# A two-pass graph kernel: the second pass's steps for loading, comparing, expanding and adding a block are set one or two turns nearer to its gather

## What is computed

```python
h = jnp.maximum(_layernorm(x, axis=-1), 0.0)
agg = jax.ops.segment_sum(h[src], dst, num_segments=h.shape[0])   # edges sorted by dst
x = x + jax.nn.relu(agg @ W.T + b)
```

## Time and profile before

| | |
|---|---|
| median of 3 runs | 1252.31 us (1250.37 to 1253.11) |
| profiled execution | 1251.71 us, of which the span is 1249.8 us |
| PE busy | 968.8 us (78%) |
| DVE busy | 1024.1 us (82%) |
| POOL busy | 784.5 us (63%) |
| ACT busy | 280.4 us (22%) |

### The profile page before, as it was taken

One profiled execution on the slowest core, in us unless ns is written; L12 is line 12 of the kernel. 1 busy time (PEld: TensorE's weight loads), 2 busy tenths in 40 slices (PEclk: granted clock), 3 DMA queues, 4 the chain that ended last, 5 costly groups with the idle time before them and its releaser, 6 DMA issues.

```text
span 1249.8 us, 20773 instructions
## 1 busy us (share of the span) xinstructions
PE 968.8 (78%) x5818; PEld 765.5 (61%) x5818; DVE 1024.1 (82%) x2720; ACT 280.4 (22%) x681; POOL 784.5 (63%) x836
## 2 busy tenths in 40 slices
PE   0122017999999999999999814888988989788988
PEld 0011014777777777777777613776776777676777
DVE  8888896899999999999999635677767777777874
ACT  1451032222222222222222111111112112111210
POOL 3000047777777777777778367777777777777750
PEclk9996556899999999999999855889898888989889
DMA  1000012788999899898897544778787777787765
GB/s 65 0 0 0 0 41 69 176 223 221 241 239 236 223 244 234 233 232 218 234 238 204 161 145 105 181 200 224 187 233 201 206 198 208 206 211 220 201 172 164
DMA packets 317563, 218.51 MB, mean 175 GB/s; under 512 B 223428, under 2 KB 255140, under 8 KB 317444
## 3 DMA queue, kind: packets, MB, share of 16 engines
q1 hardware_dynamic: 182100, 135.41, 38.6%
q10 hardware_dynamic: 110256, 62.42, 19.0%
q0 software_dynamic: 25088, 19.32, 8.7%
HBM read 137.51 MB, written 79.45 MB: 174 GB/s over the span
## 4 chain that ended last, share of the span: by engine, by line
DVE 47%; PE 16%; DMA 12%; POOL 9%; issue 7%; ACTq 6%; ACT 3%; DVEq 0%; POOLq 0%; SPq 0%
POOL xa L555 9%; DMA xa<-node_table,gi 7%; DVE feats L1077 7%; DVE feats L1075 7%; DVE oneh L1098 5%; DMA win<-records 4%; DVE dout L1117 4%; ACTq L679 4%; PE p_m L1364 3%; DVE kb L923 2%; DVE rec L1125 2%; DVE ka L923 2%; DVE shared L1098 2%; PE p_u L1376 2%; PE p_t L1376 2%
## 5 line engine op out<-in xcount | busy, mean ns | idle before, releaser
L536 POOL DMA_INDIRECT xa<-in_edge_attr_dram,gi x392 | 373.0, 952 | 232.2 <-issue 115.6
L555 POOL DMA_INDIRECT xa<-node_table,gi x392 | 370.1, 944 | 142.3 <-issue 103.1
L689 ACT ACTIVATE hid<-p_z,bias_z 128x512 f32<-128x512 f32 x98 | 113.5, 1158 | 239.3 <-issue 226.5
L1077 DVE TENSOR_TENSOR_SCAN feats<-c_rows,feats,p_g 32x512 f32<-32x512 f32 x97 | 123.3, 1271 | 1.4
L1075 DVE TENSOR_TENSOR_SCAN feats<-c_rows,feats,p_g 64x512 f32<-64x512 f32 x97 | 122.5, 1263 | 0.0
L1405 PE MATMUL p_g<-ident,hn 128*128 128x128 f32 x196 | 46.6, 325 | 97.4 <-DVE hn L1179 97.2
L742 ACT ACTIVATE sd<-mv,eps_t 128x4 f32<-128x4 f32 x98 | 29.2, 298 | 407.0 <-DVE mv L1170 350.0
L1098 DVE SCALAR_TENSOR_TENSOR shared<-p_m,node_of 112x1024 f32<-112x1024 f32 x98 | 117.2, 1196 | 3.8 <-PE p_u L1376 1.4
L1364 PE MATMUL p_m<-w_s,hid 128*128 128x64 f32 x784 | 109.3, 283 | 14.0 <-ACT hid L689 13.4
L1098 DVE SCALAR_TENSOR_TENSOR oneh<-p_m,node_of 112x1024 f32<-112x1024 f32 x98 | 119.3, 1217 | 0.2
L1381 PE MATMUL p_u<-one 128*128 128x512 f32 x230 | 115.9, 590 | 0.1
(11 more groups left out here) (257 smaller groups left out, 1577.1 us busy)
## 6 DMA issues: line engine op xcount, KB each, us to landing
win<-records SPq DMA_DIRECT2D x980, 28.9 KB
records<-rec ACTq DMA_DIRECT2D x196, 132.0 KB
din<-in_x_dram SPq DMA_DIRECT2D x49, 512.0 KB
node_table<-dout SPq DMA_DIRECT2D x49, 512.0 KB, 4.3
din<-node_table SPq DMA_DIRECT2D x43, 512.0 KB, 4.8
out_dram<-dout SPq DMA_DIRECT2D x43, 512.0 KB
c_rows<-rows_src ACTq DMA_DIRECT2D x141, 128.0 KB
win<-records ACTq DMA_DIRECT2D x588, 28.9 KB
```

The costliest lines, as they stand in the source:

```text
L536: g.indirect_dma_start(out=xa[n % XRING][:, t, 0:FE], out_offset=None, in_=edge_attr, in_offset=bass.IndirectOffsetOnAxis(ap=gi[0][:, BT * ...
L555: g.indirect_dma_start(out=xa[k % XRING][:, t, :], out_offset=None, in_=T, in_offset=bass.IndirectOffsetOnAxis(ap=gi[1][:, BT * n + t:BT * ...
L689: s.activation(hid[n % 2][:, :].rearrange("p (t n) -> p n t", n=P), p_z[n % 2][:, :].rearrange("p (n t) -> p n t", t=BT), ACT.Relu, bias=b ...
L1077: v.tensor_tensor_scan(f[64:96, :], c[64:96, at:at + BLK], p_g[n % 2][0:32, :], first[64:96], ALU.min, ALU.max).then_inc(feats_ok, 1)
```

## The change

Six of the distances change, and PE's turn is put in another order.

```diff
-DST_TAKE, DST_CONV, DST_REC, DST_WIN, DST_HOT, DST_EXP, DST_ADD, DST_PUT = 1, 2, 3, 6, 8, 9, 10, 12
+DST_TAKE, DST_CONV, DST_REC, DST_WIN, DST_HOT, DST_EXP, DST_ADD, DST_PUT = 1, 2, 3, 5, 7, 7, 8, 10
+DST_DIN = DST_ADD - 2
...
-                    if (n - DST_HOT) % 2 == 0 and valid(n - DST_HOT) and (n - DST_HOT) // 2 < ringed[1]:
-                        load_dense(1, (n - DST_HOT) // 2, T)
+                    if (n - DST_DIN) % 2 == 0 and valid(n - DST_DIN) and (n - DST_DIN) // 2 < ringed[1]:
+                        load_dense(1, (n - DST_DIN) // 2, T)
...
                 for n in range(BLOCKS + DST_EXP):
+                    if valid(n - DST_CONV):
+                        conv(n - DST_CONV)
+                    if valid(n):
+                        turn_h(n)
                     if valid(n - DST_EXP):
                         expand(1, n - DST_EXP)
                     if valid(n - DST_EXP) and valid(n - DST_EXP + 1):
                         pe.wait_ge(added, max(BLOCKS + n - DST_EXP + 1 - len(p_e[1]) + 1, BLOCKS))
                         stream(p_e[1][(n - DST_EXP + 1) % len(p_e[1])], BLK // 2)
-                    if valid(n - DST_CONV):
-                        conv(n - DST_CONV)
-                    if valid(n):
-                        turn_h(n)
```

## The result

The change made the kernel slower: 1265.73 us (median of 4 runs, 1257.96 to 1270.54) against 1252.7 us for the kernel before (four runs, where the table above has three), a ratio of 1.0107 with a 95% interval of 1.0069 to 1.0144. 1249.4 us had been forecast, in a range of 1246 to 1252.8; a slower kernel had been given one chance in ten. The profiled execution took 1265.09 us, its span is 1263.3 us against 1249.8.

A forecast was written before the change was run, and what follows sets the result against it. POOL's gathers, 1.249 us apart, were taken to pace the head and PE the tail. One expansion turn saved (-3.1) plus a tail loss (+0.2) made -2.9 us: 1249.4 us, range 1246 to 1252.8.

The forecast's parts named there:

- The tail: After the last gather, paced by PE: eight expansions left behind the last transposition, not nine, saving 3.1 us; 0.2 us lost.
- the second turn: Turn between PE's last expansion and DVE's addition: costs nothing today, so saves nothing.
- no loss for the last windows: Last windows at the pass's end, possibly held back by their records: loss between 0 and 2.0 us, taken as 0.2.
- the 35.9 given as a sign of being right: Stretch behind POOL's last gather: was to take 35.9 us, not 38.8, if the forecast was right.
- PE's moved expansion: One expansion done before the tail, about 6 us moved into PE's 94 us free in the head: cost nothing.
- the addition two turns sooner: DVE's addition, distance 10 to 8, may wait for PE's expansion: cost nothing, up to 10 us of lateness.
- the 2 us at a time: DVE's addition waiting for PE's expansion when PE is at its low clock: about 2 us.
- Windows a turn sooner: Window loads, distance 6 to 5: SP's data between 1.6 us early and 1.3 us late for the keys; cost taken as nothing.
- Dense loads and stores: The pair's load keeps two turns before its addition, the store two turns behind it: cost nothing.
- Rival C: Slower: DVE paces the head through new waits, 1268 us with 0.7 us of them a turn; chance 0.12.
- POOL's lead of 10 us: POOL's last gather came 10.3 us after the addition it needs; lateness up to 10 us was to cost nothing.

The follow-up runs named there:

- both cures: The changed kernel with the dense pair ahead of SP's windows and the dense store in another turn than the load: 1244.21 us, ratio 0.9965.
- experiment 1: The changed kernel with windows and one-hots at their distances of before (6, 8), addition at 9 and store at 11: 1249.85 us, ratio 1.0007.

## Why the prediction was wrong

*The tail* was right to a tenth: one expansion turn less, 3.1 us, the second turn worth nothing, no loss for the last windows. (Behind the last gather the changed kernel has 41.3 us, and not the 35.9 given as a sign of being right, nearly all of it the 5.1 us of lateness that PE brings along from the head.) In the kernel with both cures (1244.21, ratio 0.9965) the forecast of -2.9 us, a ratio of 0.9977, lies within the interval.

*PE's moved expansion* and *the addition two turns sooner*: cost nothing, as predicted: in the kernel with both cures POOL's 391 steps take 488.3 us (716.4 to 1204.7). DVE did wait for PE, 16.2 us between 850 and 1190, within the 2 us at a time that were worked out; experiment 1 shows that it is free.

*Windows a turn sooner* is the step that failed, in the sentence "I take nothing", together with *Dense loads and stores: Nothing*. It was seen that SP would be released by the record and not by the expansion of m-4. Only SP's windows were then followed, to find that they would be in time, and they were. What stands behind them in SP's queue was not followed: the dense pair, whose own waits had not changed but whose queue had. It was shifted onto ACT's windows, in every second turn, where before it met them at varying distances. The prediction had put a cost of 0 there; the runs show about 22 us in the head (17.0 in POOL's row, 5.1 behind its last gather). The load of the pair is also the sixth of the "six distances" of the change, from turn 8 to turn 6; it and the store kept their places in SP's turn, and that was read as keeping their times.

*Rival C* named the right place, DVE becoming the pace of the head, and had 0.12. Its price went by SP's late windows and the additions; neither is on the chain. That the growth starts only when POOL's lead of 10 us is eaten was right (POOL starts 40 or 41 gathers in each 50 us from 800 to 950 us and 38 or 39 from there to 1200), and also that windows and the rest of the turn are what DVE has to fit into 5.00 us: it needed 5.36 in the chain above (10.71 for two turns) and 5.34 on average. Put into the sum of rival C that gives 98 x 0.34 - 10 = 23 us (an estimate), against the 22 measured. What was missing was the loop over ACT. It could have been added up from the trace of before: keys are two turns behind ACT's loads, so the round is 2.7 us from the moments to ACT's first load, the landing, and 0.2 us for the keys. It exceeds 10 us once it takes more than 7.1 us from ACT's first issue to the keys. The kernel before has landings on both sides of that: ACT's loads of 949.56 us ended a wait at 954.52, after 5.0 us, and those of 953.31, which met the pair of 953.77, at 961.55, after 8.2 us:

```profile
953.31 1.84 ACTq L679 DMA_DIRECT2D win<-records  x4
953.77 0.44 SPq L397 DMA_DIRECT2D din<-node_table  x1
961.55 0.17 DVE L1088 COPY p_m<-win 112x8 f32<-112x8 f32 x1 [3.25 <-DMA win<-records]
```

There the slow ones were not a rule (by the landings in the traces, 7 of 68 blocks between 850 and 1190 us took more than 7.1 us, against 29 of 64 in the changed kernel); its 54.4 us of waits for windows were the sign of them, and I had read them as slack that nobody notices.

## What to carry to other kernels

When the event that releases a queue changes, follow everything that stands behind it in the queue, and ask which other transfers it will then start beside; the largest transfer matters most, even if it is never waited for. Find the loops that close over several turns through a DMA's landing and compare their sum with the pace of the slowest engine: a wait that costs nothing now says how near such a loop is. A step moved sooner is worth only what it takes from the end of the pass, here one turn of 3.1 us of the two; once the transfers were kept apart, the traces show that turn gone, and the times agree with it within their interval.

## What had not been expected

- With 1 MB of dense transfers started within 0.5 us of four windows of 29 KB each, it is 7.3 us from the first issue to their landing (1012.77 to 1020.04); those issued at 1007.15, with no dense transfer started within 4 us, had landed by 1011.70, after 4.55 us. Between 850 and 1190 us of the changed kernel the mean is 7.7 us (6.6 to 9.2) with the pair beside them and 5.0 us (3.8 to 6.2) without.
- The order is stable. It isn't a chance meeting that averages out: a long turn and a short one alternate (the keys at 1003.45, 1009.86, 1013.74 and 1020.56 us stand 6.4, 3.9 and 6.8 us apart), and each round puts the pair on ACT's windows again. In all 32 rounds between 850 and 1190 us the dense load starts 0.05 to 0.85 us ahead of ACT's first window; in the kernel before it lay up to 4.9 us ahead or 4.2 us behind.
- With dense transfers of 64 KB the mean granted clock of the span was 0.916, against 0.882 in the changed kernel, with the same matmuls. Why is open; nothing was run for it.
